# One key's query-key product of the four-key tiles: from VectorE to GpSimd

## What is computed

```python
xn = _layernorm(x, axis=-1)
# attention, hd = 32, scale = hd ** -0.5
qkv = xn @ Wqkv.T + bqkv                  # split into q, k, v, then into heads
scores = mask + scale * jnp.einsum('bnd,bmd->bnm', q, k)
attn = jax.nn.softmax(scores, axis=-1)
out = jnp.einsum('bnm,bmd->bnd', attn, v)
y = out @ Wproj.T + bproj
# linear branch: quantize_e4m3(xn) @ quantize_e4m3(Wffn).T + bffn
result = x + y + linear
```

## Time and profile before

| what | value |
|---|---|
| time of the runs | 1519.7, 1521.7, 1521.72 us (median 1521.7) |
| the profiled execution's own time | 1524.79 us |
| its span on the core | 1523.0 us |
| granted TensorE clock, mean | 0.993 of full speed |
| busy: TensorE, VectorE, GpSimd, ScalarE | 1482.5, 1452.9, 1320.3, 1258.3 us |

### The profile page before, as it was taken

One profiled execution on the slowest core, in us unless ns is written; L12 is line 12 of the kernel. 1 busy time (PEld: TensorE's weight loads), 2 busy tenths in 40 slices (PEclk: granted clock), 3 DMA queues, 4 the chain that ended last, 5 costly groups with the idle time before them and its releaser, 6 DMA issues.

```text
span 1523.0 us, 24295 instructions
## 1 busy us (share of the span) xinstructions
PE 1482.5 (97%) x6871; PEld 677.6 (44%) x6871; DVE 1452.9 (95%) x1220; ACT 1258.3 (83%) x2959; POOL 1320.3 (87%) x1087
## 2 busy tenths in 40 slices
PE   6999999999999999999999999999999999999997
PEld 3444444444444444444444444444444444444454
DVE  6989999999999999999999999999999999999997
ACT  5678889797897979789797987979889797988942
POOL 2578989989898998989889898998989989898984
PEclk9999999999999999999999999999999999999999
DMA  7447877969878787977969878786887969778652
GB/s 226 85 111 144 171 167 160 191 137 192 165 162 181 152 188 152 174 164 165 184 144 184 168 148 183 165 181 148 170 178 158 184 150 185 167 163 176 132 144 69
DMA packets 389478, 246.22 MB, mean 162 GB/s; under 512 B 313952, under 2 KB 313952, under 8 KB 389344
## 3 DMA queue, kind: packets, MB, share of 16 engines
q1 hardware_dynamic: 363568, 182.27, 51.3%
q0 software_dynamic: 25776, 62.40, 25.3%
HBM read 104.34 MB, written 34.08 MB: 91 GB/s over the span
## 4 chain that ended last, share of the span: by engine, by line
POOL 62%; issue 29%; PE 4%; DVE 2%; DMA 1%; POOLq 1%; ACT 0%; SPq 0%; DVEq 0%; ACTq 0%
POOL prod_pv L593 24%; POOL o L555 7%; POOL x L629 6%; POOL xs L573 6%; POOL prod_qk L564 5%; POOL rstd L624 4%; POOL probs L541 3%; POOL shifted L549 3%; POOL xs L580 2%; POOL prod_pv L656 1%; PE v_ps L973 1%; PE k_ps L973 1%; POOLq L79 1%; PE q_ps L973 1%; DMA xT<-x 1%
## 5 line engine op out<-in xcount | busy, mean ns | idle before, releaser
L593 POOL TENSOR_TENSOR prod_pv<-kv,probs 128x2048 f32<-128x2048 f32 (+1 forms) x182 | 619.0, 3401 | 9.6
L1219 DVE TENSOR_REDUCE scores<-prod_qk 128x64 f32<-128x2048 f32 x192 | 439.3, 2288 | 6.6
L1309 DVE TENSOR_REDUCE o_nat<-prod_pv 128x512 f32<-128x2048 f32 (+1 forms) x121 | 404.6, 3344 | 29.5 <-POOL prod_pv L593 10.7
L1214 DVE TENSOR_TENSOR prod_qk<-q_ps,kv 128x1536 f32<-128x1536 f32 (+1 forms) x192 | 397.9, 2073 | 0.2 <-issue 0.2
L973 PE MATMUL k_ps<-wqkv_hi,xT 128*128 128x512 f16 x1024 | 329.9, 384 | 16.3 <-DMA xT<-x 15.6
L973 PE MATMUL v_ps<-wqkv_hi,xT 128*128 128x512 f16 x1024 | 325.7, 379 | 0.0
L973 PE MATMUL q_ps<-wqkv_hi,xT 128*128 128x512 f16 x1024 | 325.4, 379 | 0.0
L973 PE MATMUL proj_ps<-wproj_hi,oT 128*128 128x512 f16 x952 | 302.6, 379 | 0.0
L711 ACT ACTIVATE prod_pv<-kv,probs 128x32 f32<-128x32 f32 x960 | 244.5, 341 | 0.0
L823 ACT ACTIVATE kv<-v_ps 128x512 f32<-128x512 f32 x128 | 140.7, 1099 | 86.3 <-PE v_ps L973 86.3
L973 PE MATMUL k_ps<-wqkv_lo,xT 128*128 128x512 f16 x512 | 196.5, 384 | 0.0
(11 more groups left out here) (173 smaller groups left out, 2160.5 us busy)
## 6 DMA issues: line engine op xcount, KB each, us to landing
xn<-in_L_attn_x SPq DMA_DIRECT2D x132, 256.0 KB, 2.8
xs<-in_L_attn_x SPq DMA_DIRECT2D x124, 256.0 KB, 2.9
out<-xs SPq DMA_DIRECT2D x124, 256.0 KB, 2.0
xs<-projected POOLq DMA_DIRECT2D x120, 256.0 KB, 4.2
xs<-out_bias POOLq DMA_DIRECT2D x59, 512.0 KB, 5.9
xT<-x SPq DMA_TRANSPOSE x256, 3.3
kv<-in_L_attn_Wqkv SPq DMA_DIRECT2D x3, 1024.0 KB, 8.1
oT<-o SPq DMA_TRANSPOSE x122, 4.2
```

The source lines that it names most:

```text
L593: nc.gpsimd.tensor_tensor(o, v, p, ALU.mult).then_inc(pv_multiplied, 1)
L1214: nc.vector.tensor_tensor(prod_qk[:, first_row:first_row + keys, :], qb, k, ALU.mult).then_inc(qk_multiplied, 1)
L1219: nc.vector.tensor_reduce(scores[:, n % 2, :, m0:m0 + 4].rearrange("p h m -> p m h"), prod_qk[:, row:row + 4, :].rearrange("p m (h d) -> p ...
L1309: nc.vector.tensor_reduce(o_nat[:, n % 2, :], prod_pv[:, place:place + units, :].rearrange("p q (c m) -> p c q m", m=4), AX_XY, ALU.add).t ...
```

## The change

The product of one key is made by GpSimd for short tiles too. ScalarE copies the query for every tile; GpSimd's `first_key` runs for every tile, in the row of the tile's parity as before; VectorE multiplies three keys instead of four in the only unit of a short tile and its reduction waits for GpSimd's row. All counts of `q_copied` and `first_key_multiplied` go from long tiles to all tiles. The diff, cut to its core (the other lines only put `tile_count` in the place of `heavy_count`):

```diff
             def first_key(i, n):
-                after(pool, q_copied, heavy_count(i, n))
+                after(pool, q_copied, tile_count(i, n))
...
-                if live(i, j, L_FIRST) and keys_of(j - L_FIRST) == N:
+                if live(i, j, L_FIRST):
                     first_key(i, j - L_FIRST)
...
-                if live(i, j, L_FIRST) and keys_of(j - L_FIRST) == N:
+                if live(i, j, L_FIRST):
                     n = j - L_FIRST
                     after(act, q_summed, tile_count(i, n))
-                    after(act, first_key_multiplied, heavy_count(i, n - 1))
+                    after(act, first_key_multiplied, tile_count(i, n - 1))
                     nc.scalar.activation(q_first[:, :], q_ps[n % 4][:, :], ACT.Copy).then_inc(q_copied, 1)
...
-                shared = keys_of(n) == N and m0 == 0
+                shared = m0 == 0
...
                 if shared:
-                    after(dve, first_key_multiplied, heavy_count(i, n))
+                    after(dve, first_key_multiplied, tile_count(i, n))
```

More of the change, by code:

```diff
@@ L649, in late_products @@
                     pool.wait_ge(qk_multiplied, units_before(TILES - N))
-                    pool.wait_ge(first_key_multiplied, heavy_count(0, TILES - N - 1))
+                    pool.wait_ge(first_key_multiplied, tile_count(0, TILES - N - 1))
                     pool.wait_ge(pv_multiplied, units_before(TILES - N))
@@ L833, in copy_query @@
                 act.wait_ge(q_summed, t + 1)
-                act.wait_ge(first_key_multiplied, heavy_count(0, t - 1))
+                act.wait_ge(first_key_multiplied, tile_count(0, t - 1))
                 nc.scalar.activation(q_first[:, :], q_ps[t % 4][:, :], ACT.Copy).then_inc(q_copied, 1)
@@ L1341, in second_products @@
                 if t >= TILES - 2:
-                    dve.wait_ge(first_key_multiplied, heavy_count(0, TILES - N - 1))
+                    dve.wait_ge(first_key_multiplied, tile_count(0, TILES - N - 1))
                     dve.wait_ge(pv_multiplied, units_before(TILES - N))
@@ L1378, in ending @@
                 for t in range(TILES - 3, TILES):
-                    dve.wait_ge(q_copied, heavy_count(0, t))
+                    dve.wait_ge(q_copied, tile_count(0, t))
                     scores_of_unit(0, t, *key_units(t)[0])
```

## The result

The change makes the kernel slower. In runs of both kernels on the same chip the median went from 1521.7 us (1519.7 to 1523.8, 6 runs) to 1531.8 us (1529.1 to 1535.4, 6 runs): a ratio of 1.0067 with a 95% interval from 1.0057 to 1.0078, or +10.1 us. The forecast was 1530 with a range of 1519 to 1543. The profiled execution of after has a span of 1530.0 us (before: 1523.0).

What follows compares the result with a forecast made beforehand. The prediction took a 90.70 us loop through VectorE and GpSimd, closing once a round, as the bound. GpSimd's loop +2.4 and ScalarE's term +5.6 make +8 us on the median of 1521.7: 1530, range 1519 to 1543.

Steps and rivals of the forecast that it cites:

- ScalarE's stretch: From TensorE's slot 0 through ScalarE's last-key products of slot 2 to VectorE's slot-3 sum: 29.90 us, 31.38 with the copies.
- GpSimd's loop: VectorE slot 0, GpSimd slots 1 and 2, VectorE's slot-3 sum to next slot 0: 90.70 us becomes 90.86, +2.4 in all.
- the first loop: GpSimd's loop, closing once a round through VectorE's slot 0 and slot 3: 90.70 us before, 90.86 with the change.
- L: Time from VectorE's slot 0 to TensorE's: taken as 1.1 us before, 2.3 after; ScalarE decides from 1.55 after the change.
- TensorE's floor: TensorE's 416 matmuls a round at 0.216 us each: no round can be shorter than 89.8 us.
- ScalarE's term: Copies and a later TensorE delay VectorE's slot-3 sum: 0.37 us a round, 5.6 us in 15 rounds (0 to 10).
- about half stays: The 0.75 us excess of L lengthens the round and shortens the next L, leaving about half: 0.37 a round.
- the growth of L: TensorE's slot 5 waits for slot 4's later transpose, so L grows by 0 to 1.75 us; 1.2 taken.
- Head and tail: The program's start and end, going by GpSimd's loop or having GpSimd idle: costed at nothing, 2 us either way.
- Rival 1: Only GpSimd's loop counts, as TensorE does not get later: +2.4 us, 1524; chance 0.21.
- Rival 2: Faster: GpSimd's loop gives way and VectorE's saving shows up until TensorE's floor, 1508, or 1515 for half; chance 0.12.
- Rival 3: TensorE's longer transpose waits lower its clock; five more rounds losing 2.6 us each add up to 13 us: 1543; chance 0.20.

Runs made afterwards that it cites:

- e4: The changed kernel with tile 2 of each round as before (VectorE multiplies four keys, no copy, no GpSimd product): 1519.6 us, ratio 0.9988 to the kernel before.
- e9: The kernel before with only tiles 0 and 3 of each round changed: 1516.5 us, ratio 0.9970.
- e11: The changed kernel with tile 3 of each round back on VectorE: 1535.7 us, ratio 1.0088 to the kernel before.
- e2: The changed kernel without GpSimd's product for short tiles; copies stay, VectorE multiplies three keys, an old row stands in: 1514.3 us, ratio 0.9958 to the kernel before.
- e10: The kernel with tiles 0, 1 and 3 moved, without ScalarE's short-tile copies except the first four tiles: 1512.3 us, ratio 0.9939 to the kernel before.
- e1: The changed kernel without ScalarE's query copy for short tiles except the first four; GpSimd multiplies an older query: 1527.3 us, ratio 1.0035 to the kernel before.
- e8: The kernel before with ScalarE's query copies for short tiles added but not used: 1525.2 us, ratio 1.0023.
- e6: The kernel before with only tile 0 of each round changed: 1514.2 us, ratio 0.9949.
- e7: The kernel before with only tiles 0 and 1 of each round changed: 1513.9 us, ratio 0.9957.

## Why e4 missed: a second loop, through TensorE

The kernel with tiles 0, 1 and 3, in two rounds that follow on each other. GpSimd writes the low half of x in slot 3 of the first:

```profile
356.69 1.15 POOL L651 TENSOR_TENSOR x<-xn,x 128x512 f16<-128x512 f32 x1
```

TensorE waits for that tile's transpose at its slot 4, and comes to the next round's slot 0 without another wait:

```profile
365.73 0.39 PE L995 MATMUL k_ps<-wqkv_hi,xT 128*128 128x512 f16 x1 [1.76 <-DMA xT<-x]
...
410.63 0.38 PE L995 MATMUL k_ps<-wqkv_hi,xT 128*128 128x512 f16 x1
```

VectorE's sum of that round waits for ScalarE, and sets the next slot 0:

```profile
441.49 4.42 DVE L1331 TENSOR_REDUCE o_nat<-prod_pv 128x512 f32<-128x4096 f32 x1 [1.78 <-ACT prod_pv L733]
...
499.42 0.68 DVE L1320 BATCH_NORM_STATS2 stats<-xn 128x6 f32<-128x512 f32 x1
```

From the first slot 0 (317.3) the steps are 39.4 to the low half of x, 9.0 to TensorE, 44.9 for its four slots, 30.9 for ScalarE's stretch (two of the copies lie in it here), 57.9 to the next slot 0: 182.1 us in two rounds, 91.05 a round, and these two lasted 90.40 and 91.71. That the steps add up to the time of two rounds is no proof, since one begins where the other ends; what tells are the two waits in the rows, TensorE's for the transpose and the sum's for ScalarE. The step from x to TensorE varies. In the five rounds of this kernel in which TensorE waits in slot 4 it is 7.3 to 9.1, 7.8 on average, and with that the loop is 90.45 a round. In the other rounds TensorE waits in slot 5, or not at all because it is still late.

The same five steps in the kernel after. From slot 0 at 411.68:

```profile
452.33 1.15 POOL L629 TENSOR_TENSOR x<-xn,x 128x512 f16<-128x512 f32 x1
```

```profile
459.60 0.39 PE L973 MATMUL k_ps<-wqkv_hi,xT 128*128 128x512 f16 x1 [1.31 <-DMA xT<-x]
...
504.80 0.38 PE L973 MATMUL k_ps<-wqkv_hi,xT 128*128 128x512 f16 x1
```

```profile
536.13 4.42 DVE L1309 TENSOR_REDUCE o_nat<-prod_pv 128x512 f32<-128x4096 f32 x1 [2.32 <-ACT prod_pv L711]
...
594.07 0.68 DVE L1298 BATCH_NORM_STATS2 stats<-xn 128x6 f32<-128x512 f32 x1
```

These are 40.65 + 7.27 + 45.20 + 31.33 + 57.94 = 182.39, or 91.2 a round, more than GpSimd's 90.86. In before the same steps are 38.7 + 7.6 + 44.9 + 29.9 + 58.5 = 179.6, or 89.8 a round, 0.9 under GpSimd's loop. (The 7.6 is the mean of after again, where TensorE waits in slot 4 in all 13 rounds; in before it waits there in four, with 7.4 to 9.6.) The change lengthens two of its steps: x comes 1.9 later by the products in GpSimd's slots 1 and 2 (less VectorE's saving), and ScalarE's stretch is 1.4 to 1.5 longer; VectorE's saving in slot 3 takes 0.5 off the last. Half of the sum, +1.4, falls on each round, and with it this loop overtakes the other.

The product of tile 3 is off GpSimd's loop, since it stands behind slot 2's second products, but it is in front of the x of slot 3, so it lengthens the second loop by half of 1.22 a round. That is why, by my account, moving tile 3 gives less than the first loop says, in e4 and e9 alike. Two other runs bear the part of x out. In e11, with tile 3 back on VectorE, x is at 39.4 instead of 40.65, L falls from 1.88 to 1.26 on average, and ScalarE is the releaser in 3 rounds instead of 12. And e2 has all four copies but x at 38.2: its mean round is 90.23, 0.34 below e4's, though its stretch is 0.5 longer. For e10 the second loop gives (39.4 + 7.6 + 44.9 + 29.9 + 57.95) / 2 = 89.9 and its mean round is 89.99, but TensorE doesn't wait in slot 4 in any of its 13 rounds and its floor of 89.8 is as near: e10 shows what the copies cost and can't tell the loop from the floor. I had drawn up e4's expectation from the first loop and TensorE's floor, without this one.

## Why the prediction was right

**GpSimd's loop: right**, to 0.04 us in every set of tiles in which it decides, with 1.22 as the price and tile 2's product alone on it.

**ScalarE's stretch: right in mechanism and price.** The copies move it from 29.90 to 31.36 (forecast 31.38). The sum starts at L + 31.3 where ScalarE decides: with L of 2.10 the sum is 33.42 after slot 0, with 2.63 it is 33.96.

**The size of ScalarE's term: right.** I gave it 0.37 a round; the sum of slot 3 starts 0.34 later than GpSimd's loop says on average (33.27 against 32.93). In 13 rounds that is 4.4 us, and e1 and e8 price the copies at 4.5 and 3.9. It came from an L of 2.3 of which half the excess was to stay, thus from a settled L of 1.55 + 0.37 = 1.92; measured is 1.88, though the prediction had named an L near 2.3 as the sign. There is some luck in it: L in before is 0.88 without the two late rounds (1.36 with them) where I took 1.1, and it grew by 1.0 where 1.1 to 1.92 is 0.8. What stood there as "about half stays" is the second loop, which I didn't close; by its rows above it gives 91.2, which is 90.86 + 0.34. I looked for the growth of L at the transpose of slot 4, where the earlier trace rows show a wait; after, it is the one of slot 3, in every round. Both are asked for 1.9 later.

**Missing: 0.14 a round behind the sum**, 1.9 us in all, most of it two waits of VectorE for an input tile (1.07 and 0.36). The prediction had no term for it, and what causes the waits stays open.

**Head and tail: mis-sized.** They were costed at nothing beyond one crossing each, 0.53. Slot 24 begins at 228.2 instead of 227.1 (+1.1), and from slot 128 to the end it is 114.4 instead of 113.0 us (+1.4).

The sum, by these: 13 rounds of 91.35 - 90.70 = 0.65 are 8.4 us, head and tail 2.5, together 10.9 against a kernel before without late rounds. The two medians differ by 10.1, the two profiled spans by 7.0 only. The profiled execution of before had three late rounds (92.17, 92.75 and 91.04, 3.9 us above 90.70 in all), and lay 3.1 above its median, as the prediction said. The forecast's 8 was thus 2 to 3 us short: the two priced terms held, and what it missed stands in the two paragraphs above.

**Rival 1** (GpSimd's loop alone, 1524) is wrong: ScalarE is the releaser of slot 3's sum in 12 of 13 rounds and GpSimd in one; e1 prices the copies at 4.5 us and e8 at 3.9. **Rival 2** (faster) would be right for other sets of tiles. It stood or fell with the product of slot 1, 1.22 against 1.06, and e4, e6, e7 and e9, which leave that product out, are all faster than before (e4 by 0.1% only). **Rival 3** (the clock) is wrong here. Between 182 and 1365 us the granted clock is as in before:

```profile
182.00:1365.00 1183.00, 1166.06 (x5388) 525.19 (x5387) 1116.88 (x932) 1044.40 (x2489) 1138.20 (x932) 1.00 0.82 168
```

TensorE does wait more (28.0 us), but in many short waits whose longest is 2.5, no longer than before (2.7).

The Trainium skill (GPSIMD Engine Reference, "Engine selection") advises against such a move, as GpSimd takes about twice as long for a product of two inputs. Here it takes 1.22 against 0.53, a factor of 2.3. The advice was right for the whole change and wrong for e6 and e7, where GpSimd's time was idle time; the factor by itself didn't decide.

## What to carry to other kernels

Price a moved instruction by the loops it lands on, not by the busy share of the engine that takes it: here the same move costs 20 us for one tile and saves 7 for another. Close every loop that goes once round all engines, also those that take two rounds to close, and divide; the slack between the first and the second tells how far a gain on the first will carry (e4). And when an edit repeats over several places, move each alone: the best version with the whole output moves the product of tile 0, or of tiles 0 and 1, and is 7 to 8 us faster than the kernel before.

## What was not expected of the hardware

**A late TensorE can cost more than its wait.** In e1 TensorE waited 3.27 us for a transpose:

```profile
838.17 0.61 PE L995 MATMUL k_ps<-wqkv_hi,xT 128*128 128x512 f16 x1 [3.27 <-DMA xT<-x]
```

Its granted clock was 0.78 over the 13 us from 838 on, in which it did 47 matmuls in place of some 60 (busy time and count of TensorE come first, the clock behind the five engines):

```profile
838.00:851.00 13.00, 12.83 (x47) 5.34 (x48) 12.77 (x11) 5.87 (x13) 7.44 (x7) 0.78 0.94 199
851.00:866.00 15.00, 14.89 (x70) 6.78 (x70) 14.74 (x12) 11.49 (x25) 13.02 (x11) 1.00 0.67 150
```

Its four slots took 51.1 us instead of 44.9, of which the wait is 3.3 and the clock the rest. The next round began with L at 8.18 and lasted 95.99 us. That one round is 5 us of this run, which was the slowest of its kernel. So the mechanism of rival 3 exists; it didn't decide the change. It shows in before too: TensorE's waits of 2.19 and 2.12 us in slot 4 were followed by 13 us at 0.87, by four slots of 46.6 us, and by the two rounds of 92.17 and 92.75. In after a wait of 2.04 us had nothing of the kind behind it:

```profile
368.30:381.30 13.00, 12.97 (x61) 5.87 (x62) 11.70 (x11) 8.56 (x17) 12.92 (x13) 1.00 0.96 207
```

**A small VectorE operation that takes 16 times as long.** In after's ending the product of probabilities (L1331 in the line numbers of before and after, 64 numbers a row) takes 0.21 us once and 3.44 the next time:

```profile
1497.74 0.21 DVE L1331 TENSOR_TENSOR q_ps<-exps,inv_sum 128x64 f32<-128x64 f32 x1
...
1506.26 3.44 DVE L1331 TENSOR_TENSOR q_ps<-exps,inv_sum 128x64 f32<-128x64 f32 x1
```

During the second GpSimd is in its products L656, during the first it is idle until 0.05 us before the end:

```profile
1497.90 0.30 POOL L541 TENSOR_TENSOR probs<-exps,inv_sum 128x64 f32<-128x64 f32 x1 [1.57 <-DVE inv_sum L1230]
...
1502.36 7.25 POOL L656 TENSOR_TENSOR kv<-kv,probs 128x2048 f32<-128x2048 f32 x2
```

It ends at 1509.70, 0.09 after GpSimd's two products (1509.61). The kernel before has the same pair, 0.21 and 3.44, so the change has no part in it. Other VectorE operations beside the same products of GpSimd kept their length: the sum L1368 with 4.36 us (4.41 with GpSimd idle) and L1355, which has one input in PSUM, with 0.74. That VectorE's operation was held up by GpSimd's is my reading; no run took those products away to test it.
